# Differential attention: the scores as bf16 products over nine stacked part pairs, the stack made by transfers through DRAM

## What is computed

```python
# h: the normalised, modulated input of the layer, [16, 256, 128]
q = h @ Wq + bq; k = h @ Wk + bk; v = h @ Wv + bv      # 16 heads of 8
lam = exp(sum(lq1 * lk1)) - exp(sum(lq2 * lk2)) + 0.8   # per head
p = softmax(lam * (q . k) / sqrt(8))                     # 256 x 256 per head
o = group_norm(p @ v)                                    # per head
x = x + gate * (o @ Wo + bo)
```

## Time and profile before

| | |
|---|---|
| median of 3 runs | 5513.1 us |
| the profiled execution | 5521.02 us, span 5519.3 us |
| TensorE busy over the span | 4929.2 us (89%) |
| VectorE, ScalarE, GpSimd busy | 71%, 61%, 48% |
| first projection of the stage to its last residual | 940.8 to 1344.8 us |
| mean granted TensorE clock over the span | 0.949 |

### The profile page before, as it was taken

How to read it: one execution, slowest core, us unless ns; L and a number is a source line. 1 busy time by engine, 2 the same in 40 slices (tenths; PEclk the granted TensorE clock), 3 DMA queues, 4 the chain that set the end, 5 groups by cost and what they waited for, 6 DMA issues and landing times. The chain is left out here.

```text
span 5519.3 us, 130512 instructions
## 1 busy us (share of the span) xinstructions
PE 4929.2 (89%) x50569; PEld 3352.3 (61%) x50569; DVE 3922.5 (71%) x6510; ACT 3359.4 (61%) x5923; POOL 2660.5 (48%) x1681
## 2 busy tenths in 40 slices
PE   6888555997899999999999999999999999799897
PEld 4444233554677667776777677766776777566544
DVE  5999797775677777777777677767777777477553
ACT  5776322554666666666666666666666666455444
POOL 4777110000566556665666566655555666266200
PEclk8999656998999999999999999999999999899898
DMA  2121000000000100010000000010001000000020
GB/s 84 61 77 62 4 0 7 2 1 19 17 12 12 29 14 11 11 30 15 11 11 20 25 11 11 12 30 12 11 11 33 12 11 11 14 2 2 24 62 19
DMA packets 76242, 113.90 MB, mean 21 GB/s; under 512 B 22496, under 2 KB 53424, under 8 KB 72048
## 3 DMA queue, kind: packets, MB, share of 16 engines
q1 hardware_dynamic: 67744, 110.60, 7.3%
q10 hardware_dynamic: 8256, 0.03, 0.1%
HBM read 70.38 MB, written 2.49 MB: 13 GB/s over the span
## 5 line engine op out<-in xcount | busy, mean ns | idle before, releaser
L2211 POOL TENSOR_TENSOR lt_qk<-lt_qk,lt_rot 128x1024 f32<-128x1024 f32 x384 | 907.0, 2362 | 207.3 <-DVE lt_rot L2575 207.3
L2221 POOL TENSOR_TENSOR lt_prob<-lt_prob,lt_total 128x1024 f32<-128x1024 f32 x192 | 365.1, 1902 | 1086.5 <-DVE lt_total L2597 1086.5
L2216 POOL TENSOR_TENSOR lt_qk<-lt_qk,lt_rnorm 128x1024 f32<-128x1024 f32 x384 | 726.2, 1901 | 110.5 <-ACT lt_rnorm L2451 102.9
L2258 PE MATMUL lt_ps<-lt_w_qk,lt_xs 128*128 128x512 f32 x1536 | 749.8, 611 | 23.0 <-DMA lt_scales<-in_L_scales 11.3
L2310 PE MATMUL lt_ps<-lt_z,lt_fold 128*128 128x256 f32 x3072 | 678.8, 379 | 1.3 <-ACT lt_z L2479 1.3
L2310 PEld LDWEIGHTS lt_ps<-lt_z,lt_fold 128*128 128x128 f32 x3072 | 583.6, 190 | 121.5 <-ACT lt_z L2479 24.4
L2572 DVE TENSOR_TENSOR lt_qk<-lt_ps,lt_table 128x1024 f32<-128x1024 f32 x384 | 467.8, 1218 | 79.0 <-ACT lt_sq L2441 72.1
L2575 DVE TENSOR_TENSOR lt_rot<-lt_ps,lt_table 128x512 f32<-128x512 f32 x768 | 490.1, 679 | 0.0
L2587 DVE TENSOR_REDUCE lt_nmax<-lt_ps 128x16 f32<-128x1024 f32 x192 | 229.9, 1197 | 360.5 <-PE lt_ps L2278 360.4
L2582 DVE TENSOR_REDUCE lt_norm<-lt_sq 128x16 f32<-128x1024 f32 x384 | 463.4, 1207 | 0.0
L2258 PEld LDWEIGHTS lt_ps<-lt_w_qk,lt_xs 128*128 128x128 f32 x1536 | 272.7, 193 | 253.9 <-issue 247.2
(11 more groups left out here) (406 smaller groups left out, 9935.5 us busy)
## 6 DMA issues: line engine op xcount, KB each, us to landing
mb_bs<-mb_rows SPq DMA_DIRECT2D x16, 1536.0 KB, 7.6
lt_xw<-lt_xw SPq DMA_DIRECT2D x192, 128.0 KB, 2.3
mb_bs<-mb_rows SPq DMA_DIRECT2D x16, 512.0 KB, 4.2
mo_gate_b<-mo_rows SPq DMA_DIRECT2D x16, 512.0 KB, 5.5
lt_xs<-h SPq DMA_DIRECT2D x96, 64.0 KB, 1.9
lt_w_qk<-in_L_ffn_Wqkv SPq DMA_DIRECT2D x6, 1024.0 KB, 4.9
lt_xs<-h SPq DMA_DIRECT2D x96, 63.8 KB, 1.9
lt_wvT<-in_L_wvT SPq DMA_DIRECT2D x6, 512.0 KB, 7.4
```

The costliest lines, as they stand in the source:

```text
L2211: pool.tensor_tensor(qk[:, u, :, :], qk[:, u, :, :], rot[:, u % 2, :, :], ALU.add).then_inc(sg["added"], 1)
L2216: pool.tensor_tensor(qk[:, u, :, :], qk[:, u, :, :], rnorm[:, u, :, :].to_broadcast([P, H, DH]), ALU.mult).then_inc(sg["qk"], 1)
L2258: last = pe.matmul(AT[u][:, 512 * k:512 * k + 512], xs[:, m.j, c:c + P], w_qk[:, a, 512 * k:512 * k + 512], start=True, stop=True)
```

## The change

- q and k are projected once per item and operand, without padding (dimension-major order of the heads), 2 products of 128x256 in place of 8; ScalarE copies both into `qk`. `key` and `shift` on VectorE are gone.
- GpSimd (`split`) makes three bf16 parts of each: cast, subtract, cast, subtract.
- SyncE (`stack`) stores the parts of q and k to DRAM and, once both have landed, loads them into `q` and `k` with 72 rows, 9 pairs by 8 dimensions: six loads of 24 rows by 8 KB. `q` and `k` have three buffers; the loads of item n wait until item n-3 has had its last `scores_turned`.
- the score products are bf16 over rows 0 to 71 (75 with the maximum), with the whole array, not a strip.
- the maximum goes the same way: `turn_max`, now once per 4 pairs, writes 8 rows, ScalarE (`copy_top`) copies, GpSimd (`split_top`) splits, SyncE (`add_top`) stores and loads 3 rows into `q`. The 3 matching rows of `k` are ones.
- the offsets move: `scores` from 3 to 10, `scores_turned` from 8 to 21, `turn_max` from 6 + 2G to 14 + 4b, `weigh` to 24 + 2G, `turn_out` to 26 + 2G, the residual from 26 to 39.

```diff
+    FIRST, SECOND = 10, 21
+    TURN_MAX = FIRST + ITEM // 2
+    VALUES, WEIGH, TURN_OUT, TURN_ITEM = SECOND - 6, SECOND + 3, SECOND + 5, SECOND + 12
+    MEAN, SQUARE, VAR, NORM, OUT, ADD = (TURN_ITEM + k for k in range(1, 7))
-    SLOTS = ITEM * (B + 4)
+    SLOTS = ITEM * (B + 5)
...
+            def stack(n):
+                sp.wait_ge(sg["split"], n + 1)
+                if n >= 2:
+                    sp.wait_ge(sg[f"stacked{(n - 2) % 3}"], 96 * ((n - 2) // 3 + 1))
+                for a in range(2):
+                    sp.dma_start(rows[n % 2, a, :, :, :, :].rearrange("i d h s -> (d h) i s"),
+                                 parts[:, n % 2, a, :, :]).then_inc(sg["stored"], 16)
+                sp.wait_ge(sg["stored"], 32 * (n + 1))
+                if n >= 3:
+                    sp.wait_ge(sg["scores_turned"], H * (n - 2))
...
+                for i in range(PARTS):
+                    at = PARTS * DH * i
+                    sp.dma_start(q[at:at + PARTS * DH, n % 3, :, :].rearrange("p h s -> p (h s)"),
+                                 rows[n % 2, 0, i:i + 1, :, :, :].rearrange("i d h s -> i d (h s)").to_broadcast([PARTS, DH, H * S])
+                                 ).then_inc(sg[f"stacked{n % 3}"], 16)
+                    sp.dma_start(k[at:at + PARTS * DH, n % 3, :, :].rearrange("p h s -> p (h s)"),
+                                 rows[n % 2, 1, :, :, :, :].rearrange("i d h s -> (i d) (h s)")).then_inc(sg[f"stacked{n % 3}"], 16)
+
+            def add_top(b):
+                n, half = divmod(b, 2)
+                sp.wait_ge(sg["top_split"], b + 1)
...
+                sp.dma_start(top_rows[b % 2, :, :, :].rearrange("i h s -> h i s"), top_parts[:, b % 2, :, :]).then_inc(sg["top_stored"], 16)
+                sp.wait_ge(sg["top_stored"], 16 * (b + 1))
+                sp.dma_start(q[TERMS:ROWS, n % 3, HALF * half:HALF * half + HALF, :].rearrange("p h s -> p (h s)"),
+                             top_rows[b % 2, :, :, :].rearrange("i h s -> i (h s)")).then_inc(sg[f"topped{b % 2}"], 16)
+
+            for slot in range(SLOTS):
+                if (n := due(slot, 2, ITEM, B)) is not None:
+                    stack(n)
+                if (b := due(slot, TURN_MAX, ITEM // 2, 2 * B)) is not None:
+                    add_top(b)
...
+            def split(n):
...
+                pool.tensor_copy(parts[:, j, :, 0, :], qk[:, j, :, :]).then_inc(sg["split_high"], 1)
...
+                pool.tensor_tensor(rest[:, :, :], qk[:, j, :, :], parts[:, j, :, 0, :], ALU.subtract).then_inc(sg["split_rest"], 1)
...
+                pool.tensor_copy(parts[:, j, :, 1, :], rest[:, :, :]).then_inc(sg["split_mid"], 1)
...
+                pool.tensor_tensor(parts[:, j, :, 2, :], rest[:, :, :], parts[:, j, :, 1, :], ALU.subtract).then_inc(sg["split"], 1)
...
             def scores(p, side, qt):
...
-                last = pe.matmul(ps_s[:, side, qt, :], q[r:r + K, j, g, qt * P:(qt + 1) * P], k[r:r + K, j, g, :],
-                                 start=True, stop=True, tile_position=(r, 0))
+                last = pe.matmul(ps_s[:, side, qt, :], q[0:TERMS, n % 3, h, qt * P:(qt + 1) * P], k[0:TERMS, n % 3, h, :],
+                                 start=True, stop=True)
...
             def scores_turned(p, side, kt):
...
+                    if p % R == 0:
+                        b = p // R
+                        pe.wait_ge(sg[f"topped{b % 2}"], 16 * (b // 2 + 1))
...
+            def turn_max(b, projected):
+                n, half = divmod(b, 2)
+                pe.wait_ge(sg["max"], R * (b + 1))
+                pe.wait_ge(sg["qk_in"], projected)
+                if b >= 1:
+                    pe.wait_ge(sg["top"], b)
...
+                if (b := due(slot, TURN_MAX, ITEM // 2, 2 * B)) is not None:
+                    turn_max(b, projected)
+                    tops += 1
+                if (G := due(slot, WEIGH, 2, GROUPS)) is not None:
+                    weigh(G)
...
-                first, second = due(slot, 3, 1, PAIRS), due(slot, 8, 1, PAIRS)
+                first, second = due(slot, FIRST, 1, PAIRS), due(slot, SECOND, 1, PAIRS)
```

More of the change, by code:

```diff
@@ L548, in shape_constants @@
     out["L3_w_oT"] = np.ascontiguousarray(T["L3_attn_w_o"].T)
[L550 to L562, removed]
+    dims_first = lambda v: v.reshape(-1, H, DH).swapaxes(1, 2).reshape(-1, H * DH)
+    out["L1_w_qk"] = np.stack([dims_first(T["L1_attn_Wq"]), dims_first(T["L1_attn_Wk"])], 1)
+    out["L1_cols"] = np.stack([T["L1_attn_bo"], T["L1_attn_gn_w"].reshape(-1), T["L1_attn_gn_b"].reshape(-1),
+                               dims_first(T["L1_attn_bq"])[0], dims_first(T["L1_attn_bk"])[0]], 1)
+    out["L1_lvec"] = np.tile(np.stack([T["L1_attn_" + name] for name in ("lq1", "lk1", "lq2", "lk2")], 1), (DH, 1, 1))
     out["L1_gmean"] = np.kron(np.eye(H, dtype=f32), np.full((DH, DH), 1.0 / (DH * S), f32))
@@ L1442, in stage_diff_attention @@
         ps_x = psum("ps_x", [P, 2, S])
-        LOADS = 8
+        LOADS = 7
         block = ctx.enter_context(nc.Block())
@@ L1464, in _ @@
+            for slot in range(SLOTS):
+                if (n := due(slot, 1, ITEM, B)) is not None:
+                    split(n)
+                if (b := due(slot, TURN_MAX, ITEM // 2, 2 * B)) is not None:
+                    split_top(b)
         @block.tensor
@@ L1469, in _, with project @@
             pe.wait_ge(sg["w_in"], 16 * LOADS)
[L1471 to L1479, removed]
+            def project(n, tops):
+                if n >= 1:
+                    pe.wait_ge(sg["qk_in"], n)
+                if tops:
+                    pe.wait_ge(sg["top"], tops)
+                for a in range(2):
+                    last = pe.matmul(ps_p[:, a, :], w[:, a, :], ln.h[:, n, :], start=True, stop=True)
+                last.then_inc(sg["qk_made"], 1)
             def values_in(n):
@@ L1599, in _, with query, copy_top @@
             act.wait_ge(sg["lsum"], 2)
-            nc.scalar.activation(lsum[:, :, :], lsum[:, :, :], ACT.Exp).then_inc(sg["lexp"], 1)
+            nc.scalar.activation(lsum[:, :], lsum[:, :], ACT.Exp).then_inc(sg["lexp"], 1)
             act.wait_ge(sg["w_in"], 16 * LOADS)
             act.wait_ge(sg["qscale"], 3)
-            def query(u):
-                n, g = u // 2, 2 * (u % 2)
-                act.wait_ge(sg["q_made"], u + 1)
+            def query(n):
+                act.wait_ge(sg["qk_made"], n + 1)
                 if n >= 2:
[L1608 to L1612, removed]
+                    act.wait_ge(sg["split"], n - 1)
+                nc.scalar.activation(qk[:, n % 2, 0, :], ps_p[:, 0, :], ACT.Identity, bias=qbias[:, 0:1], scale=qscale[:, 0:1])
+                nc.scalar.activation(qk[:, n % 2, 1, :], ps_p[:, 1, :], ACT.Identity, bias=col[:, 4:5]).then_inc(sg["qk_in"], 1)
+            def copy_top(b):
+                act.wait_ge(sg["max_turned"], b + 1)
+                if b >= 2:
+                    act.wait_ge(sg["top_split"], b - 1)
+                act.copy(top[:, b % 2, :], ps_p[0:HALF, 0, :]).then_inc(sg["top"], 1)
             def exponents(p):
@@ L1682, in _ @@
             dve.wait_ge(sg["qscale"], 2)
-            nc.vector.tensor_tensor(qbias[:, :], qscale[:, :], bias[:, 0, :], ALU.mult).then_inc(sg["qscale"], 1)
+            nc.vector.tensor_tensor(qbias[:, :], qscale[:, :], col[:, 3:4], ALU.mult).then_inc(sg["qscale"], 1)
             dve.wait_ge(sg["blank"], 2)
[L1686 to L1693, removed]
             def values_in(n):
```

173 lines of the change are left out of this document (94 added, 79 removed).

## The result

The changed kernel takes 5628.79 us in the median of 4 runs (5605.46 to 5647.44), the kernel before 5513.29 beside it: ratio 1.0201, with an interval of 1.0181 to 1.022. It is slower, by 115.5 us (2.0%); 5621 us were forecast, in a range of 5540 to 5710.

What follows compares the result with a forecast made beforehand. Half the stage's slots were held bound by the single `ps_s` buffer's ring, half by TensorE. With the clock partly down, 87 + 14.6 x 29.1 gave 512 us against 404, 108 more: median 5621 us, range 5540 to 5710.

Steps and rivals of the forecast that it cites:

- 87 + 14.6 X: Changed stage: 87 us fixed plus 14.6 items of X us each; X 29.1 with the clock partly down, 512 us.
- Before the first score: Stage start: projection, copies, `split`, store and six loads ahead of the first score; 15 to 19 us, taken as 17.
- Second scores only: Stage end: 11 slots with only second scores, bound by exponents and weighing, some 2.6 us each; 29 us.
- Slot 0: First of an item's 8 slots, bound by TensorE with one projection for four; 3.3 us at full clock.
- Slots 3 and 4: Within an item: slot 3 bound by the single `ps_s` buffer, 2.23 us; slot 4 by TensorE, 2.5, at full clock.
- The wait of `turn_max`: Slots 2 and 6: TensorE idles about 1.3 us for the maximum, other work queued behind; slots of 4.35 and 4.55.
- The step that carried the forecast: TensorE's clock in the stage: 0.75, read between measured rows of 61% busy at 0.59 and 77% at 0.84.
- The 71%: TensorE's busy share in a new item at full clock: 17.1 of 24 us.
- Clock stays down throughout: Rival: TensorE's clock at 0.50 for the whole stage; X 37, stage 627, 5736 us; chance 7%.
- clock stays up: Rival: TensorE keeps the full clock in the stage; X 24, stage 437, 5546 us; chance 18%.
- The loads are late: Rival: q loads use three DMA engines, 8.8 us late every item; X 32.8, stage 566, 5675 us; chance 12%.
- Faster: Rival: `turn_max` costs nothing, slots 2 and 6 bound by TensorE; item 20.2, stage 382, 5491 us; chance 6%.

Runs made afterwards that it cites:

- loads8: The change with its six row loads reordered so that each source begins with the dimension of 8, not 3; 5597.7 us, 1.0138 of the kernel before.
- turn_load: The change with `turn_max` one slot later and the row loads' sources beginning with the dimension of 8; 5502.6 us, 0.9972 of the kernel before.
- shallow17: turn_load with the second scores at offset 17 in place of 21; 5609.4 us, 1.0166 of the kernel before.
- before_thin: The kernel before with projections cut to a quarter for all items but the first, results wrong; 5492.0 us, 0.9952 of the kernel before.
- the repeat: The changed kernel run once more, unaltered; 5617.9 us, 1.0177 of the kernel before.
- warm: The change with two unread float32 products of 128x256 behind the scores of every odd slot; 5617.8 us, 1.0171 of the kernel before.

## Why the prediction was right

**The stage.** 512 us were forecast, 509.0 and 512.8 came. *87 + 14.6 X*: X was 29.1, the item took 29.14. The fixed part measures 88.9 (24.8 + 29.1 + 23.5 + 11.5) for 87, but its terms miss in both directions, and that they cancel is luck. **Before the first score** was mis-sized, 24.8 for 17: 3.3 to the start of `split` (2.1 taken), 3.8 of `split` (4.0), 2.8 from the stores to the first load (1.4), 15.0 of loads (at least 7.6). Second scores only took 23.5 for 29, the tail 11.5 for 14.

**The slots.** Products 0.11 us apart (1163.15 to 1163.38 for two) against 0.107. Slot 0 hot: 1150.38 to 1153.50, 3.1 for 3.3. Slots 3 and 4 hot: 1163.15 to 1167.76, 4.6 for 2.23 + 2.5. The wait of `turn_max`: 34.2 us in 32 product records, 1.07 us each (1.46 in those of the weight load), for 1.3, ahead of everything that the order puts behind it.

**The clock.** The step that carried the forecast, 0.75 between the two rows, measured 0.754. This is what the rule of the Trainium skill in "TensorE: Matmul & The Clock Gate", part 1, on oscillation describes, and the trace agrees: hot and cold slots in one item. The page's example has waits of 3 to 5 us for DMA; here shorter ones go with it, in `loads8` of 1.3 us at most on TensorE's product records from 1060 to 1300 us, with the clock at 0.74. But the forecast's reason, little work for TensorE in the odd slots, is only half of it: `turn_load` has the same odd slots, and 0.92. What tells the two apart is that in the change the waits ahead of `turn_max` and for its row come on top of those before the odd slots. With either kind left the clock is 0.71 to 0.75, with next to neither 0.92, and with waits for rows put in again (`shallow17`) 0.79.

That the number came out so close is luck in good part. The 71% was reckoned for an item at the full clock and read against two rows measured at their own lower clocks. The measured share, 77% (183.85 of 240), stood beside 0.84 in those rows and would have given X = 27.0, a stage of 481 us; it goes with 0.76 in the change. `turn_load` has 81% at 0.94 (194.85), `before_thin` 86% at 1.00.

**The rivals.** *Clock stays down throughout*, with X = 37, did not happen: 0.66 to 0.82 over single items. Nor did *clock stays up*, with X = 24: 0.57 already in the slots with first scores only (970 to 995). *The loads are late* was given as something in place of the forecast; it was there beside it. In the first item the loads took 15.0 us against 19 reckoned, and the row waits were some 20 us in all, where the rival had 8.8 in every item; that slots with the clock down would hide much of it, the text had said. "DMA: Bandwidth & Descriptors" of the Trainium skill, rules for kernel authors, gives the rule on a leading repeat; the change and `loads8` bear it out, with 15.0 against 10.3 us and three packets in flight against eight. *Faster* names the mechanism of `turn_load` rightly (`turn_max` costs nothing) and nearly its price: X 20.2, stage 382, against 21.2 and 384.9, and 19.5 to 20.2 in its items at 1.00. It takes two edits to get there, since `turn_max` a slot later makes the rows of the maximum late behind slow loads. Its total of 5491 lies 12 us under the 5502.6 measured.

**The total.** 115.5 us against a forecast difference of 108, and 99.4 in the repeat (5617.9 against 5518.5). The stage of the two traces gives 105 to 109. What is over on either side is within the spread of the runs (5605 to 5647), and nothing here ascribes it to a place.

**Still open.** Whether the 80 us that come with the clock in the pair of edits are all its doing: no run here moves the clock alone. Why the clock was lower in `loads8` (0.71) than in the change (0.75), though it waits less. Whether `warm` would gain with smaller products was not tried.

## What to carry over

When TensorE's work is cut but not its waits, price the item at both clocks and expect a clock between. The thinner projections were worth 22.6 us of stage by themselves, and the stage still grew by 105. Two waits that hide behind each other must be taken away together: 30 and 20 us alone, 115 as a pair; so where an edit that should pay moves the wait to another releaser (here from the maximum to its row), remove that one before judging. And for data that go through DRAM, look at what stands behind the large loads on the same queue, and at the first dimension of their source.

## What the runs showed that was not expected

- A store of 12 KB behind six loads landed after 10.5 us, with the better spread loads after 6.4 (`turn_load`, 1144.42 to 1150.80).
- Unread products raise the clock (0.75 to 0.84, 0.71 to 0.91, 0.92 to 0.96) and pay in one case of three.
- GpSimd takes 0.61 us for a cast of 128x512 and 1.15 for a subtraction, and no wait of TensorE is put down to it; 8 rows of 256 take 0.39 and 0.66, over half of that for a 32nd of the elements.
- Cutting the projections of the kernel before to a quarter leaves its clock at 1.00, and gives 23 us of stage and 26 of the median, more than `turn_load` does in all (15).
